# Eight batches through two transformer layers on one core: a new weight for the causal attention's steps in the interleaving of two batches

## What is computed

```python
# layer 0, per batch
h = layernorm(x) * (1 + ca) + sa
x = x + ga * attn0(h)      # 16 heads of 8, linear attention (elu + 1), projection, MLP 128-512-128 with exact gelu
h = layernorm(x) * (1 + cb) + sb
x = x + gb * experts(h)    # 8 experts: (silu(h @ Wg) * (h @ Wu)) @ Wd, all summed
# layer 1, per batch
h = layernorm(x) * (1 + ca) + sa
x = x + ga * attn1(h)      # 8 heads of 16, causal softmax over 512 keys
h = layernorm(x) * (1 + cb) + sb
x = x + gb * heads(h)      # 16 heads of 64, full softmax; values and outputs mixed by top-2 gates over 8 experts
```

```python
scores = jnp.where(causal, scores, -jnp.inf)
attn = jax.nn.softmax(scores, axis=-1)
out = jnp.einsum('bhqk,bhkd->bhqd', attn, v)
```

## Time and profile before

| | |
|---|---|
| median of 3 runs | 3138.16 us (3131.12 to 3141.55) |
| profiled execution | 3137.79 us |
| its span, first to last instruction | 3135.8 us |
| TensorE matmul busy | 2562.2 us (82%) |
| VectorE busy | 1557.9 us (50%) |
| ScalarE busy | 1389.2 us (44%) |
| mean granted TensorE clock | 0.923 |

### The profile page before, as it was taken

One profiled execution on the slowest core, in us unless ns is written; L12 is line 12 of the kernel. 1 busy time (PEld: TensorE's weight loads), 2 busy tenths in 40 slices (PEclk: granted clock), 3 DMA queues, 4 the chain that ended last, 5 costly groups with the idle time before them and its releaser, 6 DMA issues. The chain is left out here.

```text
span 3135.8 us, 43928 instructions
## 1 busy us (share of the span) xinstructions
PE 2562.2 (82%) x14892; PEld 1580.7 (50%) x14892; DVE 1557.9 (50%) x2650; ACT 1389.2 (44%) x2957; POOL 806.5 (26%) x370
## 2 busy tenths in 40 slices
PE   4884699789897898889897898978988898886376
PEld 2353346554475445654465544654456544654254
DVE  4225753536535384444735365353834457346622
ACT  0232226453454525553364624545255533653254
POOL 1003520106401181013701064011810136004500
PEclk6886899999899999999999999999999999998699
DMA  2110010102010120102101020101201021001001
GB/s 73 41 47 8 10 51 1 55 14 75 12 41 14 41 58 2 41 28 54 32 1 55 14 75 12 41 14 41 58 2 41 28 54 32 15 14 38 0 28 31
DMA packets 210733, 101.59 MB, mean 32 GB/s; under 512 B 137367, under 2 KB 189620, under 8 KB 210492
## 3 DMA queue, kind: packets, MB, share of 16 engines
q1 hardware_dynamic: 205052, 95.74, 11.0%
q10 hardware_dynamic: 5440, 2.75, 0.3%
HBM read 77.48 MB, written 20.99 MB: 31 GB/s over the span
## 5 line engine op out<-in xcount | busy, mean ns | idle before, releaser
L1510 DVE TENSOR_REDUCE nmax<-bank 128x1 f32<-128x512 f32 x512 | 342.8, 686 | 677.6 <-PE bank L972 677.2
L690 POOL TENSOR_TENSOR prod<-pv,mixv 128x1024 f32<-128x1024 f32 x184 | 598.7, 3291 | 274.4 <-ACT pv L1133 169.9
L1169 ACT ACTIVATE prT<-bank 128x512 f32<-128x512 f32 x512 | 305.7, 597 | 552.9 <-PE bank L705 547.6
L972 PE MATMUL bank<-keys,qs 64*128 64x512 f32 x1024 | 315.8, 694 | 201.3 <-ACT pr L1182 95.2
L1182 ACT ACTIVATE pr<-bank,nmax 128x512 f32<-128x512 f32 x512 | 350.0, 685 | 207.6 <-DVE nmax L1510 207.4
L629 POOL TENSOR_TENSOR rstd<-vareps,minus_half 128x4 f32<-128x4 f32 x48 | 50.0, 1042 | 1468.2 <-DVE vareps L1279 1468.1
L705 PE MATMUL bank<-ident,pr 128*128 128x128 f32 x2048 | 362.8, 304 | 38.8 <-ACT prT L1169 38.8
L705 PEld LDWEIGHTS bank<-ident,pr 128*128 128x128 f32 x2048 | 246.3, 153 | 261.8 <-issue 205.1
L1075 ACT ACTIVATE arena<-bank 128x512 f32<-128x512 f32 x256 | 152.9, 597 | 462.1 <-PE bank L817 384.8
L1008 PE MATMUL bank<-prT,vals 128*64 128x128 f32 x4096 | 301.5, 293 | 59.1 <-ACT prT L1169 59.1
L1475 DVE TENSOR_REDUCE vals<-prod 128x128 f32<-128x1024 f32 x256 | 305.1, 1206 | 32.7 <-POOL prod L690 32.7
(11 more groups left out here) (220 smaller groups left out, 3228.9 us busy)
## 6 DMA issues: line engine op xcount, KB each, us to landing
Wg<-in_L_ffn_Wg SPq DMA_DIRECT2D x64, 256.0 KB, 2.7
Wu<-in_L_ffn_Wu SPq DMA_DIRECT2D x64, 256.0 KB, 3.1
Wd<-in_L_ffn_Wd SPq DMA_DIRECT2D x64, 256.0 KB, 3.8
out_rows<-on SPq DMA_DIRECT2D x32, 512.0 KB, 2.6
onR<-out_rows SPq DMA_DIRECT2D x32, 512.0 KB, 3.9
xin<-in_L_attn_x SPq DMA_DIRECT2D x8, 256.0 KB, 4.2
mask_rows<-masko SPq DMA_DIRECT2D x8, 256.0 KB, 4.3
maskR<-mask_rows SPq DMA_DIRECT2D x8, 256.0 KB, 6.9
```

The costliest lines, as they stand in the source:

```text
L690: g.tensor_tensor(*value_piece(n), ALU.mult).then_inc(vprod_r[0], 1)
L972: pe.matmul((S0, S1)[(turn + odd) % 2][:, :], qs[half, j % 3, r, :], keys[half, p, :], start=True, stop=True).then_inc(s_ps[0], 1)
L1169: s.activation(prT[:, m % 3, :], TB[:, :], ACT.Copy).then_inc(pT_r[0], 1)
L1510: v.tensor_reduce(nmax[:, m % 2:m % 2 + 1], (S0, S1)[turn % 2][:, :], X_AXIS, ALU.max, negate=True).then_inc(nmax_r[0], 1)
```

## The change

One constant goes, and the weight of an `attn1` step is the number of its key tiles over four: 0.25 for steps with one key tile, then 0.5, 0.75 and 1. Before it was 0.35 for all. The eleven last marks, 32 to 42, get 1 each (eight steps and the three that drain the pipeline).

```diff
-HEAD1_SHARE, FINISH_SHARE = 0.35, 1.6
+FINISH_SHARE = 1.6
...
 def weight(name, m):
-    return HEAD1_SHARE if name == "attn1" and A1 < m <= E1 else FINISH_SHARE if name == "finish" else 1
+    return (1 + min((m - A1 - 1) // H1, NT - 1)) / NT if name == "attn1" and A1 < m <= E1 else FINISH_SHARE if name == "finish" else 1
```

## The result

The changed kernel takes 3108.28 us (median of 4 runs, 3102.09 to 3113.69), the kernel before beside it 3139.09 us. The ratio is 0.9909 [0.9891, 0.9927]: **0.9% faster**. In a later set of rounds it was 0.9921 [0.9906, 0.9935]. The forecast was 3123 us, half of the gain.

A forecast was written before the change was run, and what follows sets the result against it. It took TensorE, 82% busy, as bounding, idling in short waits within `heads`. Terms -12 + 0 - 2.4 + 0 - 0.6 = -15 us against 3137.8 us gave 3122.8, stated as 3123 us (chance 0.44), range 3103 to 3150.

The forecast's parts named there:

- "-12 us, bounds -18 and -6" for the spread: Attention on 26 marks instead of 16 in six weaves fills TensorE's idle time: 2.0 us each, -12 us in all.
- my bound: Upper bound for the attention's spread: ten more marks go from 0.47 to 0.17 us idle, 3.0 us a weave.
- "0" for the rest on fewer marks: Tail of `attn1`, `gates` and `attn0` on ten marks fewer cost nothing: 0 us.
- The sign that I had named: Third `heads`, head 38 to the end: taking over 3 us more than 96.5 us would show `attn0` pressed.
- the rival's sign: TensorE's waits for side results of `attn0` growing by 3.6 us a weave would decide for `attn0` pressed together.
- "-2.4 us" for the gelus: One pair of table loads lost in each of six weaves nets -0.4 us each: -2.4 us, bounds -15.4 and +6.
- The +1 us at the new place: Fourth gelu behind the last copy of `mixed`, ahead of the table load and head 58's scores: about +1 us a weave.
- "0" for the load: Load behind the second tile's rows on SyncE: input about 9.6 us behind `on`, VectorE waits under 1 us, 0 us.
- "-0.6 us" for the seventh: Seventh weave's attention, already thin, goes from 28 to 39 marks: -0.6 us, bounds -3 and +1.
- the rival with `attn0` pressed: `attn0` on fewer marks doubles TensorE's 4.6 us of waits for side results: slower, 3156 us, chance 0.12.
- The slower clock: Rival: the thinner attention stretch falls to clock 0.92, +5 us a weave, 3168 us, chance 0.03.
- The faster clock: Rival: the ten marks that get attention steps rise from clock 0.91 to 1.00, 3108 us, chance 0.11.

The follow-up runs named there:

- the early load: Changed kernel with SyncE issuing the next batch's load ahead of the second tile's rows again: 3088.25 us, ratio 0.9868; run again, 3089.68 us, 0.9860.
- the control: Against the early load kernel: attention as dense as before the change (0.407 each, marks 8 to 24), all else at that kernel's marks; 3128.08 us, 0.9989.
- the kernel with the old sum: Changed kernel with attention weights still shaped by tiles but scaled to the old sum of 12.25, so other stages stand as before: 3119.09 us, 0.9961.
- The kernel with 1.3: The early load kernel with all attention weights times 1.3, attention on about 31 marks: 3138.96 us, ratio 1.0021.
- 0.75: The early load kernel with all attention weights times 0.75, attention on about 21 marks: 3171.92 us, ratio 1.0102.
- both kernels without tables: Kernel before and changed kernel, each with Identity in place of the exact gelu: 3109.39 us (0.9926) and 3091.3 us (0.9863).
- the uniform weight: The early load kernel with all 35 attention steps weighing 23/35 each: 3106.77 us, ratio 0.9923.
- the second pair: Changed kernel and the early load kernel run again beside each other on one chip in one set of rounds: 3111.07 us and 3089.68 us.
- a shift by two marks: The 0.75 kernel with `attn0` begun two main marks later, at 56 (load weighs 3, each `attn0` mark 22/24): 3120.31 us, 0.9966.
- the uniform weights: Changed kernel, its late load kept, with all 35 attention steps weighing 23/35 each: 3126.02 us, ratio 0.9973.

## Why the prediction came out as it did

The direction, and the mechanism of the largest term, were right, and the time lies in the range. The sum was off by 15 us, and that it was not off by more is luck: the spread earned 14 to 18 us more in the six weaves than the sum had, the rest's new places and the seventh weave more too, and the late load, which the sum had at zero, took more than half of that back.

- **"-12 us, bounds -18 and -6" for the spread**: right in kind, a third of its size. In the same surroundings it earned 33.9 us in heads 7 to 37 of six weaves (760.4 against 726.5; 30.0 when the early load ran again), beyond my bound. The bound priced idle time alone, 3.0 us a weave; measured were 3.6 us against the control (85.5 to 64.2 over six) and 4.1 us against before (89.1 to 64.6). What the bound left out is busy time, 2.1 us a weave against the control, nearly all of it the clock. I had not looked for it there, since in the earlier trace rows the steps add 44.5 us of busy time in the third `heads` and 46.3 us in the seventh, as if a wider spread made it grow; but the same rows have 538 - 214 = 324 matmuls in the one and 706 - 366 = 340 in the other, 0.137 and 0.136 us each, so the larger figure only held more matmuls. The other omission is the shape. I looked at one-tile steps alone and held them against the change; that four-tile steps get one mark each was a third to a half of the spread's gain, and the kernel with the old sum shows by itself that it earns (0.9961).
- **"0" for the rest on fewer marks**: right in that nothing was lost. With the early load heads 37 to 53 take 306.7 us and heads 53 to 58 172.1 us, 478.8 in all, where before they took 482.8 us. The control, which moves only the rest and the gelus, takes 1476.0 us for the six weaves against 1486.2 us before, so both together gave some 10 us where the sum had 2.4. The sign that I had named, 3 us more than 96.5 us from head 38 on, did not appear (98.6 us behind the same head). The kernel with 1.3 loses 56 us in heads 37 to 53, but its longest waits there are not for results of `attn0`, which was the rival's sign; and 0.75, which leaves `attn0` more marks, loses 38.6 us there. So density alone isn't shown to be the cause.
- **"-2.4 us" for the gelus**: not settled. The pair's 8.2 us in heads 53 to 58 lie in busy time at another granted clock, and by idle time alone it gives nothing. The +1 us at the new place wasn't isolated: the activation itself stands there in both kernels without tables.
- **"0" for the load**: the step that failed. The 9.6 us behind `on` were for the input alone, and "VectorE waits under 1 us and nobody with it" took the maximum at 3059.0 us as the next that is due, from a stretch of the eighth `heads` where VectorE has no side work. The input itself came as computed, at 1331.88 + 4.3 = 1336.2 us, 9.3 us behind the issue of L564. But the broadcast rows came last (5.3 us from issue to landing, 11.8 us behind that issue), the wait was 1.96 us, and two marks of `attn0` stood between it and a maximum for which TensorE had the scores ready. The price is 21.4 us by the medians and 17 to 19 us by the six profiled weaves, 2 to 3 us of it in heads 37 to 53 of each weave.
- **"-0.6 us" for the seventh**: it gave 6.3 us (222.7 to 216.4), beyond -3. The control, denser there than the kernel before, has 229.5 us and the uniform weight 218.3 us, so it is the spread again; how much of it is the clock of that one stretch (0.83 before in heads 53 to 58, 1.00 after) stays open.
- **The rivals.** The slower clock didn't come: the attention's stretch stayed at 1.00, though thinner. I had taken the rule of the Trainium skill (page "TensorE: Matmul & The Clock Gate", section "Loop structure matters more than you think"), which asks for back-to-back matmuls, as one against the change; but the thinner stretch is still busy for 56.5 of its 58.7 us, so these rows neither bear that reading out nor speak against the rule. The faster clock came at heads 20 to 29 of the third weave, from 0.91 to 1.00, and heads 29 to 37 of the other weaves give it back (0.80, below): heads 7 to 37 of the six weaves have 0.95 to 1.00 before and 0.96 to 1.00 after, 0.97 on average both times. The price of the rival with `attn0` pressed was added up wrongly, too: 2.6 us and 1 us make 3.6 us a weave, 3160 us and not 3156. The time of the faster rival, 3108 us, was met to the microsecond, but by a larger spread less a late load, not by its own mechanism alone.

By the profiled executions the terms are: the rest and the gelus -10.2 us (1486.2 to 1476.0 in the six weaves), the spread -29.5 us (to 1446.5), the late load +19.2 us (to 1465.7), the seventh weave -6.3 us and everything outside +2.7 us, -24.1 us in all. They add up because each starts where the one before ends. The runs of the second pair have -25.9 and +16.6 us for spread and load, so each term is known to some 4 us. The medians have -23 to -31 us for the whole; what is between lies in the clock of single stretches, which these runs don't settle.

## What to carry to other kernels

When side work fills another stage's waits, give each piece of it a weight by its size, and as much width as its neighbours leave: spread and shape were worth 26 to 30 us in six weaves where the mean of busy engines told nothing. Then look at what stands behind the moved work, DMAs of a queue that waits above all: waits of some 1.4 us a weave on VectorE, ahead of a reduction that TensorE needs, cost some 3 us a weave, and issuing the load earlier took it back. Such a plan has no smooth optimum; a shift by two marks went with 52 us, most of it TensorE's busy time and not its idle time, so a place is to be tried, and never read from a total. A control must keep everything else as it was, in every stage that the changed constant reaches: here the seventh weave was one more.

## What the runs showed of the hardware

The same instructions in the same program run at different granted clocks from weave to weave. Heads 29 to 37 of the changed kernel, in all six:

```profile
578.70:604.10 25.40, 19.83 (x130) 0.80 0.00 1
941.30:966.30 25.00, 19.43 (x128) 0.80 0.00 1
1303.30:1325.00 21.70, 16.13 (x130) 1.00 0.00 1
1661.70:1686.70 25.00, 19.43 (x130) 0.80 0.00 1
2023.40:2048.40 25.00, 19.43 (x129) 0.80 0.00 1
2385.20:2410.20 25.00, 19.43 (x129) 0.80 0.00 1
```

The idle time is 5.6 us in each, and 3.3 us of busy time come and go with the clock: 0.80 is a stretch partly at 1.2 GHz and partly at 2.4 GHz. A reading of one weave alone would have found a gain or a loss of 3 us that is neither. The runs of one kernel lie apart in the same way: of the uniform weights' twelve, the fastest (3101.0 us) has a mean granted clock of 0.929 and the slowest (3134.7 us) 0.915.
